# The opening of a Mamba2 block with other banks, other queues and other engines

## The reference

```python
xn = layernorm(x)                                   # x: 2 sequences x 512 tokens x 512
# attention part, Mamba2 with 128 heads of 64 in 8 groups, state 128, chunks of 128 tokens
gate, xBC, dt = split(xn @ in_proj_w.T)             # 8192 + 10240 + 128 columns
x, B, C = split(silu(causal_conv4(xBC) + conv_b))
dt = clip(softplus(dt + dt_bias), 0.001, 100.0)
cs = cumsum(dt * A)                                 # in each chunk, A = -(1..128)
Ydiag = ((C B^T) * tril(exp(cs_l - cs_s))) (x dt)
states = B^T (exp(cs_last - cs) x dt);  carry = carry * exp(cs_last) + states
Y = Ydiag + exp(cs) C carry + x * D
s = rms_group(Y * silu(gate)) * norm_w @ out_proj_w.T
# feed-forward part with 4-bit weights
g = silu((silu(xn @ W1.T) * (xn @ W3.T)) @ W2.T)
return x + s * g
```

## Time and profile before

| | before |
|---|---|
| median of 3 runs | 1805.43 us (1804.45 to 1806.77) |
| the profiled execution | 1806.67 us |
| its span | 1804.8 us |
| TensorE busy | 1775.2 us |
| VectorE busy | 1433.7 us |
| ScalarE busy | 1226.1 us |
| GpSimd busy | 1261.0 us |

### The profile page before, as it was taken

The page is one execution under the profiler, slowest core; times in us unless marked ns, Lnnn a source line. Parts: engine busy times, 40 slices in busy tenths (PEclk is TensorE's granted clock), DMA queues, the critical chain, the costliest instruction groups (busy, mean ns, idle before and its releaser), DMA issues.

```text
span 1804.8 us, 30267 instructions
## 1 busy us (share of the span) xinstructions
PE 1775.2 (98%) x10325; PEld 1460.9 (81%) x10325; DVE 1433.7 (79%) x2206; ACT 1226.1 (68%) x2451; POOL 1261.0 (70%) x872
## 2 busy tenths in 40 slices
PE   6899999999999999999999999999999999999999
PEld 5688888888888888888888888888888888878877
DVE  7887888878878878878887887887887878877941
ACT  4877777767776777776777787667777777643320
POOL 4478777767877787768777787778777777675730
PEclk9999999999999999999999999999999999999999
DMA  5533243233423233233323243333333333235522
GB/s 160 180 112 106 93 129 112 93 114 110 128 95 109 98 121 114 97 108 110 127 90 121 95 130 108 94 105 129 104 95 120 106 116 106 77 107 152 156 80 94
DMA packets 122595, 202.84 MB, mean 112 GB/s; under 512 B 23056, under 2 KB 60560, under 8 KB 122192
## 3 DMA queue, kind: packets, MB, share of 16 engines
q1 hardware_dynamic: 120576, 197.06, 34.8%
q10 hardware_dynamic: 1872, 3.91, 0.6%
HBM read 193.57 MB, written 7.34 MB: 111 GB/s over the span
## 4 chain that ended last, share of the span: by engine, by line
PE 95%; DVE 2%; POOL 1%; ACT 1%; issue 1%; DMA 1%; SPq 0%; ACTq 0%; POOLq 0%; DVEq 0%
PE bank L135 17%; PE bank L137 17%; PE bank L136 17%; PE bank L504 11%; PE bank L543 7%; PE bank L591 6%; PE bank L593 6%; PE bank L592 6%; PE bank L758 3%; PE bank L641 3%; PE bank L631 1%; PE bank L612 0%; POOL yt L1422 0%; DMA x_in<-x_dram 0%; DVE x_in L1218 0%
## 5 line engine op out<-in xcount | busy, mean ns | idle before, releaser
L1418 POOL TENSOR_TENSOR yt<-yt,ec 128x384 f32<-128x384 f32 x128 | 176.6, 1380 | 338.8 <-DVE ec L1139 338.8
L1075 DVE SCALAR_TENSOR_TENSOR z<-bank,cw_all,z 128x511 f32<-128x511 f32 (+2 forms) x477 | 355.9, 746 | 11.7 <-ACT z L870 0.5
L831 ACT ACTIVATE lm<-lm,hp 128x128 f32<-128x128 f32 x1024 | 313.2, 390 | 0.8
L135 PE MATMUL bank<-xn_hi,conv_hi 128*128 128x512 f32 x640 | 262.3, 410 | 6.6 <-DVE z L1075 6.6
L1130 DVE TENSOR_TENSOR xdt<-bank,hp 128x512 f32<-128x512 f32 x128 | 88.3, 690 | 224.6 <-PE bank L641 223.5
L1109 DVE SCALAR_TENSOR_TENSOR lm<-lm,gm 128x1024 f32<-128x1024 f32 x128 | 260.4, 2035 | 3.6 <-ACT lm L831 3.6
L137 PE MATMUL bank<-xn_hi,conv_lo 128*128 128x512 f32 x640 | 252.0, 394 | 0.0
L136 PE MATMUL bank<-xn_lo,conv_hi 128*128 128x512 f32 x640 | 251.1, 392 | 0.0
L1422 POOL TENSOR_TENSOR yt<-yt,gate 128x512 f32<-128x512 f32 x128 | 227.7, 1779 | 19.3 <-POOL yt L1418 1.4
L1427 POOL TENSOR_TENSOR conv_lo<-raw_x,conv_hi 128x512 fp32r<-128x512 f32 x124 | 219.6, 1771 | 6.6 <-ACT conv_hi L771 6.6
L870 ACT ACTIVATE z<-bank,cw_all 128x512 f32<-128x512 f32 x128 | 99.1, 775 | 169.9 <-PE bank L137 169.9
(11 more groups left out here) (135 smaller groups left out, 3948.2 us busy)
## 6 DMA issues: line engine op xcount, KB each, us to landing
lm<-cs_d SPq DMA_DIRECT2D x128, 512.0 KB, 4.1
raw_x<-w_conv_dram SPq DMA_DIRECT2D x128, 256.0 KB, 3.0
ec<-e_d SPq DMA_DIRECT2D x256, 96.0 KB, 3.7
raw_g<-w_gate_dram SPq DMA_DIRECT2D x64, 256.0 KB, 2.8
raw_o<-w_out_dram SPq DMA_DIRECT2D x64, 256.0 KB, 2.7
raw_b<-w_conv_dram SPq DMA_DIRECT2D x32, 256.0 KB, 3.5
q_raw<-w1q_dram SPq DMA_DIRECT2D x10, 256.0 KB, 3.8
q_s<-w1s_dram SPq DMA_DIRECT2D x10, 256.0 KB, 4.2
```

Source lines behind the costliest of these rows:

```text
L135: pe.matmul(dst, a_hi, b_hi, start=(i == 0), stop=False)
L831: e = act.activation(lm[m % 3][:, u, :], lm[m % 3][:, u, :], ACT.Exp, bias=hp[bd.seq][:, Q_CS, k1, u:u + 1])
L1075: dve.scalar_tensor_tensor(dst[:, d:SEQ], src[:, 0:SEQ - d], cw_all[:, bd.group, pos, 3 - d:4 - d], dst[:, d:SEQ], ALU.mult, ALU.add).then ...
```

## The change

- Normalization by tiles 0-1, 2-3 and 4-7 instead of twice four.
- ScalarE's queue: only `ident` at the start; the four small loads after x tile 3 has landed. `w_dt` goes to SP's queue behind x tiles 0 to 3.
- The first gate pieces 1 to 3 are loaded at the start into tiles that are idle then (`raw_o`, `gate`), not one after the other into `raw_g`; GpSimd splits pieces 0 and 1 before anything else.
- The first two gate products go to banks `ps_y` and `ps_x`, not `ps_g`; the first comes before x tiles 4 to 7 are turned, and the steps of sequence 1 behind conv(FILL, 7).
- `cs_d` is sent when the scans are done, before `round_xn(1)`; `decays(0)` comes behind that. In step 1 `work_a` comes first, then `decays(1)`.
- The three instructions behind softplus run on GpSimd for sequence 1 (`token_steps`), and `weigh` on GpSimd for both.
- `stage_hp` and the copies to `dc_all` move from VectorE to ScalarE: `stage_hp` in `work_b` of steps 0 and 2. `turn_q(1)` comes behind `y_diag` of step 2, not ahead of the step. `send_hp` comes behind `work_b`.

```diff
+LN_TILES = [(0, 2), (2, 4), (4, 8)]
...
+        def token_steps(eng, b):
+
+            eng.wait_ge(pa, (N_SOFT + N_EXPS) * b + N_SOFT)
+            eng.wait_ge(pd, N_PD * b + 1)
+            eng.tensor_tensor(qt[Q_DT][:, half[b], :], qt[Q_DT][:, half[b], :], ecs[:, half[b], :],
+                              ALU.add).then_inc(dt_done, 1)
+            eng.wait_ge(dt_done, 3 * b + 1)
+            eng.tensor_scalar(qt[Q_DT][:, half[b], :], qt[Q_DT][:, half[b], :], DT_MIN, DT_MAX, ALU.max,
+                              ALU.min).then_inc(dt_done, 1)
+            eng.wait_ge(dt_done, 3 * b + 2)
+            eng.tensor_scalar(qt[Q_CD][:, half[b], :], qt[Q_DT][:, half[b], :], heads[:, 2:3], None,
+                              ALU.mult).then_inc(dt_done, 1)
...
+        def gate_raw_tile(group, pos):
+
+            return [raw_g[:, :], raw_o[:, :], gate[:, 2, :], gate[:, 3, :]][pos] if group == 0 and pos < 4 else raw_g[:, :]
...
+        def gate_bank(body, k):
+
+            return ps_g if body.exists() else (ps_y if k == 6 else ps_x)
...
+            sp.dma_start(wdt_raw[:, :, :], w_dt).then_inc(wdt_in, 16)
             sp.dma_start(raw_b[:, :], w_conv[0, BC_POS[0]]).then_inc(rawb_in, 16)
+            load_gate(0)
             load_x(0)
-            load_gate(0)
             for t in range(NC, TT):
                 sp.dma_start(x_in[:, t, :], x_t[t]).then_inc(x_in_s[t], 16)
+            load_gate(1)
             load_x(1)
+            load_gate(2)
+            load_gate(3)
...
                     y_diag(body, k)
+                    if body.is_number(0) and k == 2:
+                        second_values()
                     gate_mm(body, k)
...
             conv(FILL, 5)
+            gate_mm(FILL, 6)
             for t in range(NC, TT):
                 turn(t)
...
-            pe.wait_ge(pd, N_CUM + 2)
+            pe.wait_ge(wg_done, 2)
             turn_q(0)
+            pe.wait_ge(dc_done, 2)
+            gate_mm(FILL, 7)
+            extra(FILL, 6)
+            conv(FILL, 7)
+            pe.wait_ge(gev_done, 1)
             steps_dt(1, ps_y)
-            gate_mm(FILL, 6)
-            conv(FILL, 7)
-            extra(FILL, 6)
-            gate_mm(FILL, 7)
+            pe.wait_ge(gm_done, 1)
             extra(FILL, 7)
+            pe.wait_ge(gev_done, 2)
             turn_x(FILL, 7)
...
+                if n in (0, 2):
+                    stage_hp(n // 2)
...
+            def stage_hp(b):
+
+                if b:
+                    act.wait_ge(hp_out, 16 * b)
+                for q in range(NQ):
+                    act.wait_ge(qt_tr, NQ * b + q + 1)
+                    act.activation(stage[:, q, :, :, :].rearrange("p g k (j c) -> p c (g k) j", c=NC),
+                                   qt_bank[q][:, :].rearrange("p (c u j) -> p c u j", c=NC, j=2),
+                                   ACT.Copy, scale=-1.0 if q == Q_CS else 1.0).then_inc(qt_ev, 1)
...
             raw_x_conv(FILL, 5)
+            round_x(FILL, 6)
+            gate_raw(FILL, 6)
+            send_sums(0)
+            round_xn(1)
             decays(0)
...
             raw_bc(FILL, 5)
+            silu_bc(Body(0, 0, 0), 0)
             raw_x_conv(FILL, 6)
-            round_x(FILL, 6)
             first_hp()
+            silu_bc(Body(0, 0, 0), 1)
             silu_x(Body(0, 0, 0), 0)
-            silu_bc(Body(0, 0, 0), 0)
-            silu_bc(Body(0, 0, 0), 1)
-            gate_raw(FILL, 6)
+            round_x(FILL, 7)
+            work_a(FILL, 7)
+            gate_raw(FILL, 7)
             silu_x(Body(0, 0, 0), 1)
-            work_a(FILL, 7)
             raw_x_conv(FILL, 7)
-            round_x(FILL, 7)
             soft_exp(1, ps_y)
-            gate_raw(FILL, 7)
             soft_ln(1)
...
             moments(0)
             combine(0)
+            moments(1)
             norm(0)
+            combine(1)
+            norm(1)
...
-            norm(1)
+            norm(2)
+            token_steps(dve, 0)
             cumulate(0)
...
             deviation(0)
+            deviation(1)
+            split_gate(0)
+            split_gate(1)
             low_bc(0)
             low_x(0)
-            deviation(1)
-            split_gate(0)
+            deviation(2)
             low_x(1)
-            low_bc(1)
-            split_gate(1)
             split_gate(2)
             split_gate(3)
+            low_bc(1)
             low_x(2)
+            weigh(0)
             split_gate(4)
             low_x(3)
             split_gate(5)
+            token_steps(pool, 1)
```

## The result

| | before | after |
|---|---|---|
| median (20 runs each, same chips) | 1805.29 us | 1808.49 us |
| range of the runs | 1803.69 to 1807.26 | 1806.91 to 1809.59 |
| profiled execution, its span | 1806.67, 1804.8 | 1808.65, 1806.9 |
| TensorE's first output product | 91.25 us | 93.47 us |

The ratio is 1.0016, 95% interval 1.0010 to 1.0022: real, but inside the 0.2% that I had called no change. The time lies 5.5 us above the forecast and 2.0 us above its range. So the place where I looked was right: the date of that product sets the time to about 3 us, and it came 2.2 us later.

A forecast was written before the change was run, and what follows sets the result against it. TensorE, busy 98%, was taken as the bound; its first output product 2.4 us earlier turned the profiled 1806.67 us into 1804.3, and that execution's 1.24 us over the median gave 1803.0; range 1799.2 to 1806.5.

The forecast's parts named there:

- Start: Opening up to the first projection: it would start at 14.8 us instead of 15.69, a gain of 0.9 us.
- a start that gains nothing: Rival, chance 0.15: gate split locks out VectorE, first projection takes 5.1 us at 1.2 GHz, not 2.8; time 1805.8 us.
- To the scans: First projection to VectorE's scans: normalizations 4.7 us, token instructions 3.05, scans 1.37, ending at 28.2 us instead of 29.36.
- To step 0's exponentials: Scans to step 0's first exponentials: clock holds at 2.4 GHz, saving 3 us; they start at 53.0 instead of 59.02.
- The copies: Copies for DRAM on ScalarE in steps 0 and 2: 0.90 us each start to start, 3.6 us for four.
- The plain-copy rival: Rival, chance 0.32: ScalarE writes scattered elements at full pace, 2.1 us for four copies; gain 5.4 us, time 1800.0.
- Steps 0 to 2: Exponentials to x4's copy 21.5 us; first output product, waiting for the second copies, at 88.85 instead of 91.25.
- The sum: Gain of 2.4 us gives 1804.3 us against the profiled execution; less 1.24 us, its excess over the median, 1803.0.

The follow-up runs named there:

- `after_stage_dve`: The changed kernel with the eight `stage_hp` copies back on VectorE at their old places and the second values turned ahead of step 2 again: 1805.91 us, ratio 0.9995.
- `after_plain`: The changed kernel with ScalarE's copies to `stage` written contiguously, so values are stored in another order: 1804.52 us, ratio 0.9992.
- `after_warm`: The changed kernel with unread identity products on TensorE, 16 ahead of the first transposes and 8 ahead of the first projection: 1807.04 us, ratio 1.0008.
- `warm_free`: `after_warm` with most of GpSimd's gate-piece subtractions left out and its other low parts moved behind the scans: 1804.47 us, ratio 0.9991.
- `before_warm`: The kernel before with unread identity products on TensorE, 36 ahead of the first transposes and 4 behind the first four tiles: 1807.96 us, ratio 1.0015.
- `before_stage_act`: The kernel before with only the eight `stage_hp` copies moved to ScalarE in steps 0 and 2, and the store behind them: 1811.00 us, ratio 1.0028.

## Why the prediction was wrong, step by step

- *Start.* First projection forecast 14.8, measured 15.03. Right. **Its length was wrong**, forecast 2.8 and measured 5.2 us. This is the first step that failed: the sum took one of two levels for granted. I had the mechanism among the rivals ("a start that gains nothing") at 0.15, with the earlier trace rows for it. The sum took 2.8 because the kernel before did it in 2.8, although TensorE had waited 1.50 us ahead of it there too. With the change's opening, where the transposes come in pieces and a wait of 1.97 us follows, all three profiled executions (after, `after_stage_dve`, `after_plain`) show 0.43 us a matmul; with TensorE kept busy, and 0.2 to 0.65 us of waiting left, all seven show 0.23. The opening before shows either.
- *To the scans.* ReLU's end 2.6 us late by that; four normalizations 3.58 (4.7); tokens 3.7 (3.05): the sum of 128x512 met `low_bc` (1.78 us) and the product `low_x(2)` (1.40), the clamp met nothing (0.43); scans 1.37. Their end 30.4 against 28.2: 2.2 late. So the exclusion is no part of this miss, since the forecast had it at 7.75 us and it took 7.2. It hides the clock's price: with the projection on time (`after_warm`) the three token instructions met more of GpSimd's work and took 4.6 us.
- *To step 0's exponentials.* "TensorE reaches this point 0.5 us before, so the clock should hold": it waited 1.94 us, the clock fell after the projection's first four matmuls, and the second B-C projection was copied at 37.34, 4.7 us after its start instead of 2.8. **Second failed step**, 1.9 us. From that copy on ScalarE's list took 13.9 us to the |.| (forecast 13.8) and 5.88 to the exponentials (5.8). So 2.2 + 1.9 are the 4.1 us. The wait by itself isn't the cause: `after_warm` waited 1.82 us at this place and stayed at 2.4 GHz, while `after_plain` and `after_stage_dve` waited 1.98 and 2.23 and fell, like the change. What differs ahead of it is the low first projection and the shape of the start. That `warm_free` comes to 52.67 doesn't bear out the 53.0: its scans ended 2.6 us earlier than forecast and its list behind them was longer.
- *The copies.* Starts at 65.41, 66.27, 67.19 and 68.11, and the next instruction at 69.03: 3.62 us for four against 3.6, a term of the right size. The 0.90 is in part luck: it was added up from a plain copy and a cost of the stride of 0.36 us, where the durations show 0.52. The plain-copy rival (0.32) was wrong on ScalarE; what it said plain copies would be worth, 3.0 us, lies between the 2.5 us net of the product's date and the 4.0 of the medians (`after_plain`).
- *Steps 0 to 2.* Right: 21.55 against 21.5 us, the longer wait for the state, the clock at 0.51 behind it, the wait of 1.16 us for `stage`. x4's copy to output product 14.8 us against 14.35: of the two ends of the sum the later one came, with x5's projection at 1.2 GHz, and the product waits for the end of the fourth copy, which is 1.10 us long.
- *The sum.* 1804.3 + 4.1 + 0.5 behind x4's copy = 1808.9 us for the profiled execution; measured 1808.65. The rest of the 5.5 us is no step of the kernel: I took 1.24 us off because the execution before lay above its median, and the one after lies only 0.2 above its own. Two small slips in the forecast's sum nearly cancel: its terms to the scans add to 28.4 and not 28.2, and the middle of 88.2 and 89.3 is 88.75.

The range failed because it priced the lost clock at 2.3 us (the first projection alone) and let no second loss follow it. In the three profiled executions of the changed opening the low first projection and the low second B-C projection came together, and in those with TensorE kept busy and GpSimd's order as in the change both were gone; that the one brings the other is argued from this, not shown by itself. That all of the 4.1 us is the clock's price isn't shown either: taking the clock's loss away gave back 1.8.

What stays open: what sets the level of the first projection, and what the new prologue alone is worth. The start varies by 0.7 to 1.0 us between profiled executions of the same opening, so single dates are good to about that.

## What to carry to other kernels

Ask of a moved operation how often the receiving engine's list is paid on the chain: eight strided copies on the engine that paces steps 0 to 2 cost 7 us against plain ones on VectorE, though one is only 0.3 us longer by itself (0.90 against 0.60 start to start). Put GpSimd's subtractions beside VectorE instructions that read one input from a bank, not beside scans, two-tile sums and products or fast one-input ones. Price a projection behind a wait at both levels of the clock unless a row of the same opening shows which it gets, and look whether filler on TensorE ends before the data arrive: here it brought the first projection from 0.43 to 0.23 us a matmul, and in `before_warm` it cost 1.9 us.

## What of the hardware was not expected

- *The level at the start isn't a property of the kernel.* The kernel before did its first projection at 0.23 us a matmul; `before_stage_act`, with the same opening instruction for instruction, took 16.16 to 20.70, mostly at 0.43. The Trainium skill (TensorE: Matmul & The Clock Gate, Part 1: The HAM clock gate) says that the number of matmuls at the lower clock differs from run to run of one kernel; these two rows agree. Over the 92 executions of the kernel before that were timed beside these runs, those whose mean granted clock was 0.999 took 1804.5 us (median of 20) and those at 0.996 1807.0 us (24); the changed kernel's 20 lie at 0.995 to 0.997. The profiled execution before is one of the 0.996 ones. A forecast must carry both levels for that projection, 2.4 us apart; but the loss need not arrive. In `before_stage_act` the projection ended 2.0 us later than before and step 0's exponentials came at 58.54, 0.5 us earlier.
- *Scans suffer too:* 3.80 us for four of 128x128 beside two subtractions of GpSimd, 1.37 without; and 2.40 for the four of step 1 in the changed kernel.
- *GpSimd's share of the token steps was dearer than I looked for:* the clamp of 128x512 took 2.78 us and the product 2.16, where the sum took 1.27 and VectorE needs 0.43 and 0.49 for the two. VectorE's products on `lm` ran beside them; how much of it is waiting no run tells. No wait on the chain for it shows in this profile.
